# Attention step over a pair of heads and 512 tokens, with probabilities times v in front of the query projection in even steps

## What is computed

```python
h = layernorm(x)                                   # x: 32 batches, 64 tokens, 512 wide
q = rmsnorm((h @ Wq.T), q_norm_w)                  # 32 heads of 128
k = rmsnorm((ctx @ Wk.T), k_norm_w)                # 8 key/value heads, each for 4 query heads
v = ctx @ Wv.T
p = softmax(q @ k.T / sqrt(128) + mask)            # 64 x 64 in each batch and head
x = x + tanh(g_xattn) * ((p @ v) @ Wo.T)
x = x + tanh(g_ffn) * moe(layernorm(x))            # 16 experts, top 2, and a shared expert
```

## Time and profile before

| | us |
|---|---|
| median of 3 runs | 1478.57 (1478.54 to 1479.4) |
| profiled execution | 1493.04 |
| its span in the trace | 1491.2 |
| PE busy | 1443.6 (97%) |
| DVE busy | 856.2 (57%) |
| ACT busy | 505.3 (34%) |
| POOL busy | 313.4 (21%) |

### The profile page before, as it was taken

One profiled execution on the slowest core, in us unless ns is written; L12 is line 12 of the kernel. 1 busy time (PEld: TensorE's weight loads), 2 busy tenths in 40 slices (PEclk: granted clock), 3 DMA queues, 4 the chain that ended last, 5 costly groups with the idle time before them and its releaser, 6 DMA issues.

```text
span 1491.2 us, 30893 instructions
## 1 busy us (share of the span) xinstructions
PE 1443.6 (97%) x10637; PEld 1225.6 (82%) x10638; DVE 856.2 (57%) x1848; ACT 505.3 (34%) x1129; POOL 313.4 (21%) x329
## 2 busy tenths in 40 slices
PE   6999998999999999999999999999998999899986
PEld 5888887888888888888888888888887788677764
DVE  4444446565666656666565665656788651344457
ACT  4333343333333333333333333333332501222220
POOL 1222223112121121212212121121212000333352
PEclk9999999999999999999999999999999999999997
DMA  6544431111111011111111111111122234655465
GB/s 207 175 120 134 120 114 36 39 32 44 35 35 39 32 39 39 35 37 34 39 33 41 35 35 39 32 39 47 61 75 83 93 124 180 224 165 167 142 196 171
DMA packets 91524, 125.36 MB, mean 84 GB/s; under 512 B 7840, under 2 KB 56992, under 8 KB 90976
## 3 DMA queue, kind: packets, MB, share of 16 engines
q1 hardware_dynamic: 85168, 104.16, 21.7%
q0 software_dynamic: 6320, 20.71, 4.9%
HBM read 87.36 MB, written 37.49 MB: 84 GB/s over the span
## 4 chain that ended last, share of the span: by engine, by line
PE 90%; DVE 5%; issue 2%; DMA 2%; another core or an unknown queue 1%; ACT 0%; POOL 0%; SPq 0%; DVEq 0%; POOLq 0%
PE ps L503 22%; PE ps L505 21%; PE ps L504 21%; PE ps L781 5%; PE ps L569 5%; PE ps L609 4%; PE ps L797 3%; PE ps L578 2%; PE ps L595 2%; PE ps L776 1%; DVE acc L1436 1%; PE ps L550 1%; DMA acc<-in_wv 1%; DMA wgu<-in_w_gu 1%
## 5 line engine op out<-in xcount | busy, mean ns | idle before, releaser
L430 POOL TENSOR_TENSOR qr<-qv,mhalf 128x8 f32<-128x8 f32 x64 | 105.2, 1643 | 733.0 <-DVE qv L1136 733.0
L503 PE MATMUL ps<-hT,w0h 128*128 (+2 forms) x640 | 198.4, 310 | 0.9 <-DVE w0l L1069 0.9
L504 PE MATMUL ps<-hT,w0l 128*128 (+2 forms) x640 | 195.6, 306 | 0.0
L505 PE MATMUL ps<-hT,w0h 128*128 (+2 forms) x640 | 195.4, 305 | 0.0
L1121 DVE TENSOR_TENSOR acc<-ps,acc 128x512 f32 (+1 forms) x129 | 88.7, 688 | 144.1 <-PE ps L505 144.1
L945 ACT CAST ah<-ps 128x256 fp32r<-128x256 f32 x256 | 83.4, 383 | 256.5 <-PE ps L505 253.9
L1127 DVE TENSOR_TENSOR al<-ps,ah 128x256 fp32r<-128x256 f32 x256 | 96.1, 418 | 98.5 <-ACT ah L945 98.2
L503 PE MATMUL ps<-hT,w1h 128*128 (+1 forms) x512 | 147.2, 287 | 0.0
L504 PE MATMUL ps<-hT,w1l 128*128 (+1 forms) x512 | 144.7, 283 | 0.0
L505 PE MATMUL ps<-hT,w1h 128*128 (+1 forms) x512 | 144.6, 282 | 0.0
L503 PEld LDWEIGHTS ps<-hT,w0h 128*128 128x128 f32 x640 | 122.5, 191 | 7.8 <-DVE w0l L1069 1.1
(11 more groups left out here) (222 smaller groups left out, 3150.8 us busy)
## 6 DMA issues: line engine op xcount, KB each, us to landing
wraw<-in_w_att SPq DMA_DIRECT2D x64, 256.0 KB, 2.6
ybuf<-ye SPq DMA_DIRECT2D x47, 256.0 KB, 2.0
vbuf<-vo SPq DMA_DIRECT2D x16, 512.0 KB, 3.3
kbuf<-ko SPq DMA_DIRECT2D x16, 512.0 KB, 3.8
kt<-kbuf SPq DMA_DIRECT2D x64, 128.0 KB, 2.0
vt<-vbuf SPq DMA_DIRECT2D x64, 128.0 KB, 2.0
wgu<-in_w_gu SPq DMA_DIRECT2D x4, 2048.0 KB, 8.0
craw<-in_ctxT SPq DMA_DIRECT2D x9, 512.0 KB, 4.7
```

Source lines behind the costliest of these rows:

```text
L430: pool.tensor_tensor(qr[:], qv[:], mhalf[:, 0:8], ALU.pow).then_inc(q_rt, 1)
L503: pe.matmul(dst, l_hi, r_lo, start=first, stop=False)
L504: pe.matmul(dst, l_lo, r_hi, start=False, stop=False)
L505: return pe.matmul(dst, l_hi, r_hi, start=False, stop=last)
```

## The change

The 64 steps stay, but a step now takes one *pair* of heads over *512* tokens (two chunks, a pair `d`), where it took four heads over 256. Even steps have the first pair of heads, odd steps the second. `q_head` streams 512 columns at a time into a bank of its own, so that a step has 24 matmuls of 512 columns in place of 48 of 256. The transposed probabilities of two steps are collected in `pt`, twice as large; only when an odd step's are there can `probs_v` run for the four heads: for the first 256 tokens in the odd step, where it stood, and for the last 256 at the front of the following even step, ahead of the query projection. The output projections follow one step later than before. `kt` holds 512 tokens and is loaded once in two steps, in odd ones, behind the load of the weight slice. The first step has no product and no output projection; the end of the loop has one more of each than before. The last group of steps is written out instead of looped on SP, ACT and DVE, and the order of DVE's work after the last step follows the later projections.

```diff
-            kt = sb("kt", [P, CB, S], F32, a)
+            kt = sb("kt", [P, 2 * CB, S], F32, a)
...
-            def next_loads(i, x_tiles=None):
-
-                sp.wait_ge(s_done, i + 1)
-                sp.dma_start(kt[:].rearrange("p b t -> p (b t)"), kbuf[i + 1]).then_inc(kt_in, 16)
-                sp.wait_ge(v_split, 2 * i + 2)
-                sp.dma_start(vt[:].rearrange("p b t -> p (b t)"), vbuf[i + 1]).then_inc(vt_in, 16)
-                if x_tiles is not None:
-                    x_tiles()
+            def next_loads(d, odd, x_tiles=()):
+
+                i = 2 * d + odd
                 sp.wait_ge(w_hi, i + 8)
                 sp.wait_ge(w_lo, i + 8)
                 sp.dma_start(wraw[:], w_att[i + NC]).then_inc(wr_in, 16)
...
+                if odd:
+                    sp.wait_ge(s_done, i + 1)
+                    load_k(d + 1)
+                for n in x_tiles:
+                    if n >= 2:
+                        sp.wait_ge(x1_done, n - 1)
+                    sp.dma_start(xt3[n % 2][:], x[n]).then_inc(x3_in[n % 2], 16)
+                sp.wait_ge(v_split, 2 * i + 2)
+                sp.dma_start(vt[:].rearrange("p b t -> p (b t)"), vbuf[i + 1]).then_inc(vt_in, 16)
...
-            def q_head(hp, h, chunk, w):
-
-                for k in range(KD):
+            def q_head(h, hp, pair, w, ks=range(KD)):
+
+                for k in ks:
                     c0 = k * 512 + (2 * hp + h) * P
-                    hc = [hT[:, bass.ds(chunk, 1), x_, k, :].rearrange("p a t -> p (a t)") for x_ in range(2)]
-                    mm = split_product(pe, PS[hp][:, h * CT:(h + 1) * CT], w[0][:, c0:c0 + P],
-                                       w[1][:, c0:c0 + P], hc[0], hc[1], k == 0, k == KD - 1)
+                    hc = [hT[:, bass.ds(2 * pair, 2), x_, k, :] for x_ in range(2)]
+                    mm = split_product(pe, PS[h][:], w[0][:, c0:c0 + P], w[1][:, c0:c0 + P], hc[0], hc[1],
+                                       k == 0, k == KD - 1)
                 return mm
...
+            def step(d, odd, pair_q, w_q, w_before, w_o, q_ready=None, o_ready=None, first=False):
+
+
+                i = 2 * d + odd
+                if not odd and not first:
+                    probs_v(i - 1, 1)
                 if q_ready is not None:
                     pe.wait_ge(w_lo, q_ready)
                 pe.wait_ge(q_sq, 2 * i + 1)
-                q_head(0, 0, chunk_q, w_q)
-                q_head(0, 1, chunk_q, w_q).then_inc(q_done, 1)
+                q_head(0, 1 - odd, pair_q, w_q).then_inc(q_done, 1)
                 pe.wait_ge(q_sq, 2 * i + 2)
-                q_head(1, 0, chunk_q, w_q)
+                q_head(1, 1 - odd, pair_q, w_q, (0, 1))
                 transpose_probs(i)
-                q_head(1, 1, chunk_q, w_q).then_inc(q_done, 1)
-                probs_v(i)
-                scores(i + 1)
+                q_head(1, 1 - odd, pair_q, w_q, (2, 3)).then_inc(q_done, 1)
+                if odd:
+                    probs_v(i - 1, 0)
+                pe.wait_ge(pT_evac, 2 * i + 2)
+                scores(d + odd, 1 - odd)
                 q_sums(i + 1)
...
+                if not first:
+                    outputs(i - 1, w_before, w_o, o_ready)
...
-                a_hi_tile(i, 0)
-                a_hi_tile(i, 1)
+                if not first:
+                    a_hi_tile(i - 1, 0)
+                    a_hi_tile(i - 1, 1)
                 split_slice(i, w, sl)
                 exps(i + 1)
```

More of the change, by code:

```diff
@@ L320, in next_loads @@
                 sp.dma_start(wraw[:], w_att[i + NC]).then_inc(wr_in, 16)
[L322 to L335, removed]
+                if odd:
[7 more added lines that the diff above has]
+                sp.dma_start(vt[:].rearrange("p b t -> p (b t)"), vbuf[i + 1]).then_inc(vt_in, 16)
+            with sp.Fori(0, (STEPS - NC) // 2) as d:
+                for odd in range(2):
+                    next_loads(d, odd)
+            for t in range(NC - 1):
+                next_loads((STEPS - NC) // 2 + t // 2, t % 2, {0: (), 1: (0, 1), 2: ()}.get(t, (2 * t - 4, 2 * t - 3)))
             sp.wait_ge(w_hi, STEPS + 7)
@@ L338, in _ @@
             sp.dma_start(wraw[:], w_att[STEPS - 1 + NC]).then_inc(wr_in, 16)
-            for n in range(2 * (NC - 2), NT):
+            for n in range(2 * (NC - 3), NT):
                 sp.wait_ge(x1_done, n - 1)
@@ L574, in q_sums @@
                 pe.wait_ge(q_sq, 2 * j + 2)
-                squares = sq[:].rearrange("p a b h s -> p (a b) (h s)")
                 for r in range(4):
-                    rows = slice(32 * r, 32 * r + 32)
-                    mm = pe.matmul(PS[2][rows, 0:256], ones32[:], squares[:, :, rows], start=True, stop=True)
+                    s0 = 32 * (r % 2)
+                    mm = pe.matmul(PS[2][32 * r:32 * r + 32, 0:256], ones32[:], sq[:, r // 2, :, s0:s0 + 32],
+                                   start=True, stop=True)
                 mm.then_inc(ss_done, 1)
@@ L637, in _ @@
+                pe.wait_ge(pT_evac, 2 * i + 2)
+                scores(d + odd, 1 - odd)
+                q_sums(i + 1)
+                if not first:
+                    outputs(i - 1, w_before, w_o, o_ready)
             pe.wait_ge(w_lo, 4)
[L638 to L641, removed]
+            for h in range(2):
+                q_head(h, 0, 0, W[0]).then_inc(q_done, 1)
+            scores(0, 0)
@@ L642, in _, with group @@
             pe.wait_ge(acc_zero, 4)
             q_sums(0)
[L644 to L647, removed]
+            def group(d0, p, first=False, last=False):
+                i0 = 2 * d0
+                step(d0, 0, 0, W[p], W[1 - p], W[1 - p], first=first)
+                step(d0, 1, 1, W[p], W[1 - p], W[p], o_ready=i0 + 8)
+                with pe.Fori(0, NC // 2 - 2) as t:
+                    step(d0 + 1 + t, 0, t + 1, W[p], W[p], W[p])
+                    step(d0 + 1 + t, 1, t + 2, W[p], W[p], W[p])
+                step(d0 + NC // 2 - 1, 0, NC // 2 - 1, W[p], W[p], W[p])
@@ L648, in group @@
                 if not last:
-                    step(i0 + NC - 1, 0, W[1 - p], W[p], W[p], i0 + 12, i0 + 8)
+                    step(d0 + NC // 2 - 1, 1, 0, W[1 - p], W[p], W[p], q_ready=i0 + 12)
+            group(0, 0, first=True)
             with pe.Fori(0, KVH // 2 - 1) as gg:
                 for p in range(2):
[L653 to L657, removed]
@@ L909, in _, with q_out, squares @@
             act.wait_ge(hT_lo, NT)
[L912 to L918, removed]
+            def q_out(h, j):
+                act.wait_ge(q_done, 2 * j + 1 + h)
+                act.copy(qs[:, h].rearrange("p b s -> p (b s)"), PS[h][:]).then_inc(q_copy, 1)
+            def squares(h, j):
                 act.wait_ge(ss_done, j + 1)
[L920 removed]
+                act.activation(sq[:, h].rearrange("p b s -> p (b s)"), PS[h][:], ACT.Square).then_inc(q_sq, 1)
             def exps(j):
@@ L926, in exps, with probs_hi @@
                         s_exp, 1)
-            for hp in range(2):
-                q_out(hp, 0)
-                squares(hp, 0)
+            for h in range(2):
+                q_out(h, 0)
+                squares(h, 0)
             split_first(range(4, 8))
             exps(0)
-            def probs_hi(i):
+            def probs_hi(i, hp):
                 act.wait_ge(pT_done, i + 1)
-                for bp in range(2):
-                    act.copy(pt[0][:, bp, :], PS[2 + bp][:, 0:HG * S]).then_inc(pT_hi, 1)
+                for q in range(2):
+                    act.copy(pt_view(0, q, hp), pT_view(q)).then_inc(pT_hi, 1)
             def a_hi_tile(i, bp):
@@ L950, in split_slice, with act_step @@
                          w[0][:, sl * 512:(sl + 1) * 512], wraw[:]).then_inc(w_hi, 1)
-            def act_step(i, w, sl):
+            def act_step(d, odd, w, sl, first=False):
+                i = 2 * d + odd
                 act.wait_ge(s_done, i + 1)
@@ L972, in _ @@
             act.copy(g_hl[:, :, 0:E], graw[:].rearrange("p (k e) -> p k e", k=KD)).then_inc(g_hi_ok, 1)
[L973 to L978, removed]
+            for t in range(NC - 1):
+                act_step((STEPS - NC + t) // 2, t % 2, W[0], t)
+            probs_hi(STEPS - 1, 1)
+            a_hi_tile(STEPS - 2, 0)
+            a_hi_tile(STEPS - 2, 1)
+            split_slice(STEPS - 1, W[0], NC - 1)
             a_hi_tile(STEPS - 1, 0)
             a_hi_tile(STEPS - 1, 1)
-            split_slice(STEPS - 1, W[0], NC - 1)
             for n in range(NT):
@@ L1182, in residual, with dve_step @@
                 dve.bn_stats(st, row).then_inc(st_done, 1)
-            def dve_step(i, w, sl, tile, tile_before, complete=(None, None)):
-                probs_lo(i)
+            def dve_step(d, odd, w, sl, tile_before, tile, complete=(None, None), first=False):
+                i = 2 * d + odd
+                probs_lo(i, odd)
                 if complete[0] is not None:
                     residual(complete[0], 1)
-                a_rest(i, 0)
+                if not first:
```

(32 more changed lines are left out.)

130 lines of the change are left out of this document (76 added, 54 removed).

## The result

The changed kernel takes 1546.75 us (1543.26 to 1547.12, 4 runs), the kernel before 1478.89 us beside it: 1.0448 times as long, 95% interval 1.0431 to 1.0465. That is 67.9 us more; forecast were 56.5 more, 1535, in a range of 1508 to 1556. The two profiled executions, whose rows are shown, differ by only 53.8 us (1493.04 and 1546.79), because the one of the kernel before lies 14 us above its median. That excess isn't in the loop, where two steps take 28.82 to 28.84 us throughout; its cause isn't placed.

The account below looks back on a forecast made before the run. TensorE (PE) was taken as the bound inside the loop. Terms -18.6 + 43.4 + 26.4 + 4.5 were given as +56, rounded to +56.5, on a median of 1478.57: 1535 us, range 1508 to 1556.

Parts of the forecast that it names:

- The wait for k: Odd-step scores: k, issued behind the weight slice, lands late; 1.4 us each, 43 us lost (s: first query matmul's start).
- The wait for the copy: Even-step scores wait for ACT's query copy, 0.85 us each, 26 us lost (X: last query matmul's start).
- Part 2: Order in odd steps: transposes at s + 4.08, s being the first query matmul's start; costs nothing, 0.2 us cover.
- part 1: Query projection: 48 matmuls of 256 columns become 24 of 512, winning 0.30 us a step, 18.6 us.
- part 4: Even steps: probabilities times v before the query projection no longer hide ACT's copy before the scores; 26 us lost.
- The ends: First step and stage end: second softmax's wait 3 us, residual tiles at the end 1.5; 4.5 us lost.
- The figure of the Trainium skill: Query projection: fixed cost of about 2.5 ns per warm matmul, so merging would win only about 4 us.
- rival D: Query projection: the split 512-column stream costs as two matmuls do, nothing won, 1554 us; chance 0.10.

Follow-up runs that it names:

- experiment 2: Changed kernel with half of the first output projection (6 of 12 matmuls) put between query projection and scores in even steps: 1529.9 us.
- Experiments 6 and 7: Changed kernel with, first, even-step probabilities times v right before the transposes, 1540.6 us; second, two extra small matmuls before the odd-step query projection, 1547.16 us.
- experiment 4: Changed kernel with k loaded before the weight wait and, in even steps, half an output projection before scores and probabilities times v right before transposes: 1482.52 us.
- experiment 8: Changed kernel with earlier k load, even-step half projection before scores, product before transposes, and the wait for evacuated transposed probabilities behind that half projection: 1472.89 us.

## Why the prediction was right, and where it was short

**The direction and its two reasons** hold. The wait for k was put at 1.4 us in an odd step, 43.4 in all; taking it away gave 40.4, and its records add up to 39.8. The landing was taken as 2.9 us and is 2.9. The issue came at s + 5.46, inside the bounds. The wait for the copy was put at 0.80 to 0.85; the trace has the scores at X + 1.15 (664.32 to 665.47) where a run without wait would have them at X + 0.32, so 0.83 us, and experiment 2 shows that other work covers it. The sum itself was added up with a slip: its four terms give 55.7, not 56.5.

**Part 2** held: transposes at s + 4.08, no wait for DVE in the middle of the loop, probabilities times v at s + 6.00 against s + 5.97.

**The step that was mis-sized is the gain of part 1** (18.6 us, 0.30 in each step), with part 4's "the price lies where they stood before", which put the price of the product's new place at nothing. In an odd step the 18 matmuls won what I had worked out. In an even step the product in front broke the run from output to query projection: the projection and the change to the product take 5.70 us instead of 5.59, the 18 matmuls 4.26 instead of 4.08, and the piece from the transposes on 1.92 instead of 1.89 in both kinds. Together 0.11 + 0.18 + 2 x 0.03 = 0.35 us in two steps, 11 us in 31 pairs, of 18.6 expected. I had carried the change of shape (0.09) into the scores' start and had looked for no price in front. The row to see it was in the trace of before: behind the sums, the first twelve projection matmuls take 2.87 us (641.37 to 644.24 in the earlier trace rows), the next twelve 2.72. Experiments 6 and 7 put this on the break itself: moving the product to the transposes gives 6.2 of the 11 us back, and two small matmuls elsewhere make 4.24 of 4.08.

**The ends** were put at 4.5 us. In the start, the second softmax's wait is 2.25 us (3 forecast). At the end, PE waits 4.8 us for DVE's rest of the transposed second layernorm, and 1.8 before: 3 us more, where I had 1.5. Together 5 us, a little above my middle value and inside its bounds.

These add up: +42.5 (31 x 1.37, with 0.09 for the restart beside 1.28) + 25.7 (31 x 0.83) - 18.6 + 10.9 + 5 = +65.5 of 67.9. What is left, 2.4 us, was put to no test. The traces show one thing that the forecast had at nothing, the clock at the start of the stage (length, busy time by engine, granted clock, DMA share, GB/s), before and changed:

```profile
225.00:243.00 18.00, 14.20 (x115) 12.01 (x114) 11.17 (x25) 5.38 (x13) 8.61 (x7) 0.91 0.12 37
```
```profile
225.00:243.00 18.00, 13.03 (x78) 9.07 (x76) 10.52 (x22) 4.19 (x10) 7.17 (x5) 0.81 0.07 22
```

Behind the first softmax's wait, of 4.0 us, the granted clock of the changed kernel is 0.58 from 235 to 240 us, where it was 0.89; behind the second one's, of 2.25 us, it is 0.66 from 245 to 250, where it was 1.00. PE is busy for nearly all of both stretches, so this is about 3 us, an estimate from these shares (5 x 0.31 + 5 x 0.34). It may hold the rest, which isn't shown.

**The figure of the Trainium skill that was weighed** (TensorE: Matmul & The Clock Gate, "Wait — 56ns, not 53.3ns?") would have left 4 us of gain in part 1. The trace doesn't agree: 36 matmuls of 256 columns took 4.31 us, and 18 of 512 in their place take 4.08, so each that falls away saves 0.013 us, not 0.0025. The 512-column matmuls run every 0.2267 us in the odd steps, two-piece operand or not, so rival D is out too. The larger matmuls bring this saving for each one that falls away, less the price of the breaks between unlike blocks.

## What to carry to other kernels

Before a load is moved in a DMA queue, look for the wait that stands in front of it in its new place, and compare that wait's time, plus issue, plus landing, with the first use: a queue that is idle most of the time can still be late by its order. Whatever is moved away from between a producer and its consumer was cover; name what covers the pair afterwards. When matmuls are merged into larger ones to save their fixed cost, keep blocks of the same shape next to each other, put a block that breaks a run where the run is broken anyway, and put a wait directly in front of the first instruction that needs it.

## What the runs showed of the hardware

Leaving a run of 128-row matmuls costs more than the gap at the change. PE's records and its weight loads (PEld) behind the product, in the changed kernel, and then in the middle of a run:

```profile
658.25 0.28 PE L619 MATMUL ps<-pth,vth 64*128 64x256 f32 x2
658.46 0.19 PEld L512 LDWEIGHTS ps<-hT,w1h 128*128 128x128 f32 x1
658.46 0.50 PE L512 MATMUL ps<-hT,w1h 128*128 x1
658.57 0.19 PEld L513 LDWEIGHTS ps<-hT,w1l 128*128 128x128 f32 x1
658.80 0.40 PE L513 MATMUL ps<-hT,w1l 128*128 x1
...
659.04 0.40 PE L514 MATMUL ps<-hT,w1h 128*128 x1
```
```profile
641.57 0.19 PEld L512 LDWEIGHTS ps<-hT,w1h 128*128 128x128 f32 x1
641.80 0.39 PE L512 MATMUL ps<-hT,w1h 128*128 x1
```

In a run, the load of the next weights begins 0.23 us before its matmul. Behind the break it begins with it: the first matmul is followed after 0.34 us, and the next ones come every 0.23 to 0.24 until the spacing is 0.227 again, at full granted clock. The Trainium skill says (TensorE: Matmul & The Clock Gate, "Step-by-step: what each phase is for") that the engine pulls weight loads ahead of running matmuls, when the row groups don't conflict or the load goes to the background buffer. The trace agrees in that loads run ahead of their matmul inside a run. That none runs ahead across this change of shape is what the rows add; the section doesn't say it. That the late first load is what slows the matmuls behind it fits the rows but wasn't tested apart from the break; the runs show the price: about 0.1 us at the change and 0.16 to 0.18 over the next 18 matmuls of 512 columns (0.11 of it at the first).

A wait in front of a block, met about when PE reaches it, had a like price, though the list of PE's waits doesn't show it. In experiment 4 the rest of the probabilities is written at 665.81, and the first weight load of the half projection begins at 665.93, together with its matmul (665.94). In experiment 8, with the wait moved behind the block, that load begins at 663.12, 0.22 us ahead of its matmul (663.34). The even step became 0.25 us shorter on average, by the 7.7 us in the loop (in the pair shown, 28.44 us instead of 28.72, the latter from 653.27 to 681.99 in experiment 4).
